# A two-layer kernel whose first layer takes its products for two batches in three rounded parts, in a new order of calls

## The reference

```
# layer 1, xn = layernorm(x)
q, k, v = xn Wq' + bq, xn Wk' + bk, xn Wv' + bv
attn = ((elu(q) + 1) * cumsum((elu(k) + 1) * v) / 4) Wo' + bo
xr = rms(xn) * norm_w;  logits = xr Wc' / temperature          # 512 logits for a token
w = softmax of the 32 largest logits;  e = sum of w * genes      # genes: 512 x 32
x = x + attn + tanh(e Wd') * xr * (e Wu') * scale
# layer 2, xn = layernorm(x)
q, k, v = rms(xn) w_qkv';  w = exp(rms(k))
y = sigmoid(rms(q)) * cumsum(w v) / (cumsum(w) + 1e-6)
u, g = y w_swiglu';  attn = xn + (u * silu(g)) w_out'           # 1024 wide inside
moe = sum over the 2 best of 16 experts of p * down(silu(gate) * up)   # 176 wide
      + a shared expert of the same form, 352 wide
x = x + attn + moe
```

## Time and profile before

| what | value |
|---|---|
| time, median of 3 runs | 539.07 us |
| the runs | 539.32, 539.07, 535.23 us |
| the profiled execution | 531.5 us |
| its span, from first to last instruction | 529.7 us |
| mean granted clock of PE | 0.994 of full speed |
| PE busy | 507.5 us, 96% of the span |
| DVE, ACT, POOL busy | 354.0, 296.0, 272.7 us |

### The profile page before, as it was taken

How to read it: one execution, slowest core, us unless ns; L and a number is a source line. 1 busy time by engine, 2 the same in 40 slices (tenths; PEclk the granted TensorE clock), 3 DMA queues, 4 the chain that set the end, 5 groups by cost and what they waited for, 6 DMA issues and landing times.

```text
span 529.7 us, 7444 instructions
## 1 busy us (share of the span) xinstructions
PE 507.5 (96%) x2488; PEld 384.8 (73%) x2488; DVE 354.0 (67%) x735; ACT 296.0 (56%) x577; POOL 272.7 (51%) x207
## 2 busy tenths in 40 slices
PE   7989999988999999999997999999999999999995
PEld 5565577766577766877885888887777777777684
DVE  4999995786998998847899895743232323323347
ACT  3788798785767758767653636225343343424321
POOL 0475648383472373383256346464576576666510
PEclk9999999998999999999999999999999999999999
DMA  8900031026020001037001850583322232223267
GB/s 271 372 6 1 1 124 37 0 100 220 1 80 40 1 1 41 1 129 243 1 1 44 292 179 14 187 232 98 108 91 89 71 100 83 97 80 89 71 242 265
DMA packets 19813, 54.32 MB, mean 103 GB/s; under 512 B 3312, under 2 KB 5792, under 8 KB 19776
## 3 DMA queue, kind: packets, MB, share of 16 engines
q1 hardware_dynamic: 15264, 41.52, 22.7%
q0 software_dynamic: 4512, 12.33, 7.7%
HBM read 36.14 MB, written 17.74 MB: 102 GB/s over the span
## 4 chain that ended last, share of the span: by engine, by line
PE 74%; DVE 15%; DMA 4%; issue 3%; ACT 2%; POOL 1%; SPq 1%; DVEq 0%; POOLq 0%; ACTq 0%
PE bank L280 52%; PE bank L442 9%; PE bank L355 3%; PE bank L474 2%; PE bank L501 2%; DMA fa<-in_x 2%; DMA ga<-y_rows 2%; DVE tk L972 1%; DVE m L970 1%; PE bank L328 1%; DVE fe L1029 1%; PE bank L400 1%; PE bank L292 1%; DVE tk L978 1%; DVE rw L1235 1%
## 5 line engine op out<-in xcount | busy, mean ns | idle before, releaser
L1214 DVE TENSOR_TENSOR m_h<-m_h,bank 128x176 f32<-128x176 f32 x47 | 15.8, 337 | 82.9 <-ACT m_h L789 82.9
L280 PE MATMUL bank<-mw,m_xt 128*128 x188 | 66.4, 476 | 0.2
L1362 POOL DMA_INDIRECT y_rows<-m_y,dest x47 | 46.9, 997 | 30.7 <-DVE m_y L1221 20.9
L1356 POOL DMA_INDIRECT xg<-xn_rows,tab x47 | 45.5, 969 | 28.0 <-PE bank L474 19.3
L280 PE MATMUL bank<-yhr,wsg_h 128*128 128x512 f32 x128 | 56.0, 437 | 0.8 <-ACT fc L721 0.8
L280 PE MATMUL bank<-hyr,wsg_h 128*128 128x512 f32 x128 | 50.1, 392 | 0.0
L280 PE MATMUL bank<-yhr,wsg_l 128*128 128x512 f32 x128 | 50.1, 391 | 0.0
L280 PE MATMUL bank<-mw,m_ht 88*128 x188 | 48.3, 379 | 0.0
L280 PE MATMUL bank<-fe,w_qkv 128*128 128x512 f32 x96 | 44.5, 594 | 0.6 <-ACT fe L622 0.6
L1347 POOL TENSOR_TENSOR hs0r<-hs,hq0r 128x512 fp32r<-128x512 f32 (+1 forms) x17 | 23.4, 1374 | 39.8 <-ACT hq0r L776 39.8
L280 PEld LDWEIGHTS bank<-mw,m_ht 88*128 88x128 f32 x188 | 35.2, 189 | 11.1 <-issue 0.4
...
## 6 DMA issues: line engine op xcount, KB each, us to landing
...
```

The source lines that it names most:

```text
L280: mm = e.matmul(o, a, b, start=n == 0, stop=n == len(terms) - 1)
L1214: e.tensor_tensor(m_h[j % 3][:, :], m_h[j % 3][:, :], ps("ju", j)[:, 176:352], ALU.mult).then_inc(s["jh"], 1)
L1356: e.indirect_dma_start(out=xg[j % 3][:, :], out_offset=None, in_=xn_d, in_offset=bass.IndirectOffsetOnAxis(ap=tab[:, j:j + 1], axis=0)).th ...
L1362: e.indirect_dma_start(out=y_d, out_offset=bass.IndirectOffsetOnAxis(ap=dest[:, j:j + 1], axis=0), in_=m_y[j % 3][:, :], in_offset=None).t ...
```

## The change

1. For batches 2 and 3 `project` and `logits` take three products of rounded parts instead of plain f32. The high parts of the weights (kv0h, q0h, wch) are made by `split(k)` on ACT, three calls of 128x1024, 128x512 and 128x1024; the low parts by `lows(k)` on POOL, three calls of the same sizes, written over the plain weights, so each waits until batches 0 and 1 have used these. xcopy1 rounds for these batches, and `lowx(b, h)` on DVE, four calls of 128x512, makes the low part, from turn1's bank, which is free only then.
2. The two exponentials get tiles of their own, three TS and two TE, in the room of the three TK and of what is left of them. `expert` of tile n now waits until tile n-2 is turned and totalled.
3. `awake` can take another bank; there are 55 idle products (10, 2, 12, 3, 3, 2, 4, 4, 9, 6) instead of 35 (10, 2, 2, 5, 4, 2, 8, 2).
4. refine waits for one semaphore instead of two; the returns of the spilled residual (rback) wait for batch 3's projections and logits, and eround for batch 2's or 3's, as they share room with the new parts.
5. All five lists of calls are in another order.

```diff
+        TS = [tile(f"tw{n}", 512) for n in range(3)]
+        TE = [tile(f"te{n}", 512) for n in range(2)]
+        qkv0_q = tile("qkv0_q", 512, F32R)
...
+        SPLITS = [(qkv0[:, :, D:768], kv0h, qkv0l[:, :, D:768]), (qkv0[:, :, 0:D], q0h, qkv0l[:, :, 0:D]), (wcv, wch, wcl)]
...
             def project(b, j, n, first, sem, back, key):
...
+                if b < 2:
+                    q.wait_ge(s["xc1"], 2 * b + 2)
+                    terms = [(qkv0[:, c, m * P:(m + 1) * P], FE[b % 2][:, c, :]) for c in range(2)]
+                else:
+                    q.wait_ge(s["xlo"], 2 * b - 2)
+                    q.wait_ge(s["wdr"], 4)
+                    terms = []
+                    for c in range(2):
+                        wh = kv0h[:, c, (m - 2) * P:(m - 1) * P] if first else q0h[:, c, m * P:(m + 1) * P]
+                        terms += [(wh, FEr[b % 2][:, c, :]), (qkv0l[:, c, m * P:(m + 1) * P], FEr[b % 2][:, c, :]), (wh, FGr[b % 2][:, c, :])]
...
+                    for c in range(2):
+                        h, l = FEr[b % 2][:, c, t], FGr[b % 2][:, c, t]
+                        terms += [(h, wch[:, c, :]), (h, wcl[:, c, :]), (l, wch[:, c, :])]
...
+            def split(k):
...
+                raw, h, _ = SPLITS[k]
+                e.activation(h, raw, ACT.Copy).then_inc(s["bor"], 1)
...
             def expert(b, i):
                 exponent()
                 n = 4 * b + i
-                if n > 2:
-                    q.wait_ge(s["emt"], n - 2)
+                if n > 1:
+                    q.wait_ge(s["emt"], n - 1)
+                    q.wait_ge(s["to"], n - 1)
...
+            def lowx(b, h):
+                q.wait_ge(s["wcs"], 2 * b - 2)
+                q.wait_ge(s["wv"], 2 * b - 2)
+                q.wait_ge(s["xc1"], 2 * b + h + 1)
+                t = slice(h * D, (h + 1) * D)
+                e.tensor_tensor(FGr[b % 2][:, :, t], ps("t1", b, h)[:, :].rearrange("p (c t) -> p c t", c=2), FEr[b % 2][:, :, t].bitcast(F32), ALU.subtract).then_inc(s["xlo"], 1)
...
+            def lows(k):
+
+                q.wait_ge(s["bor"], 4 + k)
+                for m, n in ((s["k"], 4), (s["v"], 4), (s["q"], 4 * (k == 1)), (s["lg"], 8 * (k == 2))):
+                    if n:
+                        q.wait_ge(m, n)
+                raw, h, l = SPLITS[k]
+                e.tensor_tensor(l, raw, h.bitcast(F32), ALU.subtract).then_inc(s["wdr"], 1)
```

More of the change, by code:

```diff
@@ L517, in tensor @@
-            ffn(1, 2, 0); dgate(0, 0, 4); ffn(1, 3, 3); dup(0, 0, 5); meank(0, 0); oproj(1, 0, 3); oproj(1, 1, 4); vproj2(0, 0, 5); vproj2(0, 1, 0)
-            dgate(0, 1, 2); ddown(0, 0, 6, 7); dup(0, 1, 1); turnr(1, 0, 3); turnr(1, 1, 4); dgate(0, 2, 5); qproj2(1, 0, 3); qproj2(1, 1, 0)
-            turn2(1, 0, 4); turn2(1, 1, 2); dup(0, 2, 1); meanq(1, 4); gates(1, 2); kproj2(1, 0, 5); kproj2(1, 1, 1); meank(1, 2); vproj2(1, 0, 4)
-            ddown(0, 1, 6, 7); vproj2(1, 1, 3); dgate(0, 3, 0); turn1(2, 0, 2); dup(0, 3, 5); logits(2, 0, 1); ddown(0, 2, 6, 7); logits(2, 1, 4)
@@ new lines, in tensor @@
+            dgate(0, 4, 2); turnr(1, 0, 4); turnr(1, 1, 1); dup(0, 4, 0); ddown(0, 2, 6, 7); turn1(2, 0, 4); qproj2(1, 0, 1); logits(2, 0, 3)
+            qproj2(1, 1, 4); turn2(1, 0, 5); logits(2, 1, 2); turn2(1, 1, 0); meanq(1, 5); dgate(0, 5, 0); ddown(0, 3, 6, 7); turn1(2, 1, 5)
+            kproj2(1, 0, 1); kproj2(1, 1, 4); logits(2, 2, 3); dup(0, 5, 5); meank(1, 0); vproj2(1, 0, 2); ddown(0, 4, 6, 7); kproj(2, 0, 5)
+            kproj(2, 1, 0); vproj2(1, 1, 1); dgate(0, 6, 5); emturn(2, 0, 4); logits(2, 3, 2); dup(0, 6, 0); ddown(0, 5, 6, 7); emturn(2, 1, 3)
@@ L1244, in vector @@
-            uptimes(1, 1); uptimes(1, 2); uptimes(1, 3); dtanh(0, 0); dtimes(0, 0); khat(0, 0); khat(0, 1); joined(1, 0); joined(1, 1); stats2(1)
-            wsum(0, 0); shift2(1); wsum(0, 1); divisor(0); gateb(0); wvtimes(0, 0); rlow(1, 0); wvtimes(0, 1); rlow(1, 1); wvsum(0, 0); wvsum(0, 1)
-            dtanh(0, 1); dtimes(0, 1); refine(0); dtanh(0, 2); dtimes(0, 2); gatea(1); qhat(1, 0); qhat(1, 1); gateb(1); stats1(2); khat(1, 0)
-            khat(1, 1); ratio1(2); wvtimes(1, 0); wvtimes(1, 1); wsum(1, 0); wvsum(1, 0); wsum(1, 1); divisor(1); topa(2, 0); wvsum(1, 1); topb(2, 0)
@@ L1256, in vector @@
-            rscale(3); uptimes(3, 0); gatea(2); dout(0, 1); uptimes(3, 1); uptimes(3, 2); uptimes(3, 3); qhat(2, 0); qhat(2, 1); joined(3, 0)
-            joined(3, 1); stats2(3); dtanh(1, 2); dtimes(1, 2); gateb(2); shift2(3); khat(2, 0); khat(2, 1); dtanh(1, 3); dtimes(1, 3); wvtimes(2, 0)
-            wvsum(2, 0); dtanh(1, 4); wsum(2, 0); wvtimes(2, 1); dtimes(1, 4); wsum(2, 1); wvsum(2, 1); divisor(2); dtanh(1, 5); gatea(3); gateb(3)
-            dtimes(1, 5); routea(); rlow(3, 0); dtanh(1, 6); rlow(3, 1); dtimes(1, 6); routeb(); qhat(3, 0); qhat(3, 1); dtanh(1, 7); dtimes(1, 7)
@@ L1272, in vector @@
[L1272 to L1275 removed]
+            statsh(); stats1(0); start(); ratio1(0); wcfold(); topa(0, 0); stats1(1); topb(0, 0); topa(0, 1); tope(0, 0); topb(0, 1); topf(0, 0)
@@ new lines, in vector @@
+            vtimes(1, 0); topg(1, 1); rlow(0, 0); rlow(0, 1); topb(1, 2); tope(1, 2); vtimes(1, 1); kvsum(1, 0); topf(1, 2); kvsum(1, 1); topg(1, 2)
+            qhat(0, 0); qhat(0, 1); topa(1, 3); topb(1, 3); qplus(1); tope(1, 3); topf(1, 3); topg(1, 3); khat(0, 0); khat(0, 1); wvtimes(0, 0)
+            wsum(0, 0); wvtimes(0, 1); wsum(0, 1); divisor(0); wvsum(0, 0); rscale(1); wvsum(0, 1); gatea(0); elow(1); dtanh(0, 0); uptimes(1, 0)
+            dtimes(0, 0); uptimes(1, 1); refine(0); dtanh(0, 1); uptimes(1, 2); uptimes(1, 3); dtimes(0, 1); dtanh(0, 2); dtimes(0, 2); joined(1, 0)
@@ new lines, in vector @@
+            joined(1, 1); stats2(1); shift2(1); stats1(2); ratio1(2); gateb(0); rlow(1, 0); rlow(1, 1); dtanh(0, 3); lowx(2, 0); dtimes(0, 3)
+            dtanh(0, 4); dtimes(0, 4); topa(2, 0); topb(2, 0); tope(2, 0); topa(2, 1); topb(2, 1); topf(2, 0); qhat(1, 0); qhat(1, 1); topg(2, 0)
+            tope(2, 1); lowx(2, 1); dtanh(0, 5); topf(2, 1); topa(2, 2); topg(2, 1); topb(2, 2); dtimes(0, 5); tope(2, 2); khat(1, 0); topf(2, 2)
+            khat(1, 1); topg(2, 2); wvtimes(1, 0); wsum(1, 0); kplus(2); wsum(1, 1); dtanh(0, 6); divisor(1); dtimes(0, 6); wvtimes(1, 1); wvsum(1, 0)
@@ new lines, in vector @@
+            khat(3, 1); onehot(5); wsum(3, 0); dtanh(2, 2); counts(); wsum(3, 1); dtimes(2, 2); divisor(3); dtanh(2, 3); dtimes(2, 3); onehot(6)
+            wvtimes(3, 0); wvtimes(3, 1); wvsum(3, 0); wvsum(3, 1); dtanh(2, 4); dtimes(2, 4); dtanh(2, 5); dtimes(2, 5); refine(3); dtanh(2, 6)
+            dtimes(2, 6); onehot(7); dtanh(2, 7); dtimes(2, 7); dtanh(2, 8); dtimes(2, 8); dtanh(2, 9); places(); table(); dtimes(2, 9); dtanh(2, 10)
+            dtimes(2, 10); dtimes(3, 0); dout(2, 0); dout(2, 1); dtimes(3, 1); dlow(3, 0); jtimes(0); jtimes(1); jtimes(2); jtimes(3); jout(0)
```

370 lines of the change are left out of this document (191 added, 179 removed), and 4 rows, old and new, of the table SIGNALS.

## The result

The changed kernel takes **554.71 us** (median, 552.08 to 555.9) against 539.2 us of the kernel before (535.23 to 540.48): **1.032 times as long, 95% interval 1.027 to 1.037**. The forecast was 531, its range ended at 542. The profiled execution of the kernel after took 554.54 us, its span is 552.7; that of before was 529.7, so the spans lie 23.0 us apart.

What follows compares the result with a forecast made beforehand. PE was taken as the bound, busy 507.5 of 529.7 us. Removed products -6.9, front -2.1 and routing +0.5 sum to -8.5 us, from the median 539.07 to 531; range 523 to 542.

Steps and rivals of the forecast that it cites:

- the removed work: Plain projections and logits of batches 2 and 3 on PE: 20 groups, 0.345 us less each, 6.9 us less work.
- walk: Call-by-call pass through the new lists up to dgate(0,3), with durations from the earlier trace; it put that start near 115.2.
- even at 123.7: Start of dgate(0,3), in us, at which the change would neither gain nor lose; each us later than 115.2 costs one.
- y of batch 0 returns no earlier: Rival: late DVE waits hold refine(0), so dgate(0,3) starts at 130.7 as before; +7.0 us, 546; chance 0.13.
- the one that the products are no faster: Rival: weight loads hold the twenty groups at 1.72 us; -1.6 us left, 537.5; its 0.02 within the first rival's chance.
- so I cost this at nothing there: Added rounding on ACT, POOL and DVE from 130.7 to 280: hidden in free engine time, 0 us.
- the front and DVE take part of it back: Rival: POOL's new subtractions hold up DVE ahead of PE; gain only 2.5 to 4.9 us, 534 to 536.5; chance 0.25.
- the term's own ceiling: Added rounding, if its cover is gone: at most the operations themselves, 0.7 to 2.7 us.
- a net 2.1 us: Front: dgate(0,3) starts 15.5 us earlier, but 13.4 us of batch 1's second-layer work now stands behind it.
- no PE wait over 1 us between 130 and 260: Sign to look for in the profile after, on PE's dense part behind the front, if the prediction holds.
- The idle products: 55 for 35 on PE, 0.43 us each, 8.6 us: 6.0 in the front, 2.6 at the routing.
- the last 26.6 us ... nothing in it is changed: Tail of returns and additions behind the last expert product: kept whole, no gain or loss.

Runs made afterwards that it cites:

- lows(2) alone: Changed kernel with POOL's lows(2) held until batch 1's second norm is through on DVE, nothing else held: 536.09 us, 1.010 to the kernel before.
- its hybrid: Changed kernel up to the first xturn, every engine's list in the order of the kernel before from there: 545.68 us, 1.015 to the kernel before.
- the last two kernels: Changed kernel with lows(2), prep(4), residual(3) held and six fewer idle products: 545.49 us, 1.014; the same with the old order from the first xturn: 539.26, 1.0036.

## Why the prediction was wrong

**What held.** The groups of parts are nearly as fast as read from the earlier trace rows: six of batch 1's second layer 1.37 us apart (134.76 to 136.13), the first logits of batch 2 from 133.30 to 134.76, 1.46. The mean of the twenty groups is 1.42, of the plain ones that went 1.69, so that the removed work is 5.5 us and not 6.9. The front's move came out nearly as walked: refine(0) at 104.94 (walk 100.2, bound 106), ylow's end at 117.12 (115.3), dgate(0,3) at 119.0 (115.2, even at 123.7, wrong from 122). lows(1) ended at 82.90, before the squares for kfold(0) at 84.92. The rival "y of batch 0 returns no earlier" is out, and so is the one that the products are no faster.

**The step that failed first: "so I cost this at nothing there", for the added rounding.** It was priced by the free time of engines over 150 us. What counts is which DVE step stands beside POOL's subtraction, and who waits for it. The rival "the front and DVE take part of it back" had the mechanism (its own terms give -2.4 to -4.4 us, not the -2.5 to -4.9 that stand there), but bounded each hold-up by the one in the earlier trace rows, 1.0 us, near the length of one POOL operation. The runs show that it isn't bounded by one operation: 5.87 us, through three. Its price by the experiments: 3.0 to 4.2 us for lows(2) alone, where the term's own ceiling was 2.7; and of the products' 6.9 us only 1.8 to 3.0 are left at the first xturn. The Trainium skill (SBUF — State Buffer, Who interferes with whom) has the shared port pair with one holder at a time; the traces agree, and go beyond what was drawn from it, in that the wait lasted until POOL had a gap.

**The second: "a net 2.1 us" for the front, and "no PE wait over 1 us between 130 and 260".** The move was summed only to dgate(0,3). The list behind it is new too, and it has waits of its own, three of over 1 us between 119 and 280 and two ahead of 52 us, which the walk's durations from before couldn't hold. Four of the five (35.38, 51.15, 126.19, 278.75) stand behind a DVE step lengthened by POOL; for the first it is the same kind of step as at 117.19, 128x4 in size:

```profile
32.87 1.23 DVE L928 SCALAR_TENSOR_TENSOR sm<-mv,sm 128x4 f32<-128x4 f32 x1
```

```profile
32.81 1.27 POOL L1358 TENSOR_TENSOR te<-te,tw 128x512 f32<-128x512 f32 x1 [1.69 <-ACT tw L721]
```

Only the one at 222.46 lies between 130 and 260. Expected were about -10 us of waits and lost clock up to the experts; PE's idle time rose by 2.5 and the low clock gave back 1.7. The idle products are the half of the sum that came true (9.5 us of PE's time, 8.6 forecast), and the gain that they were set against did not. Taken away they bring nothing, since the waits are there; with the waits mended, six fewer bring 0.4 us.

**The third: "the last 26.6 us ... nothing in it is changed", and beside it the experts' stage, taken over whole.** The tail held. The stage ahead of it, 286.1 to 503.1, was booked as 0.21 us of idle PE time that stays; but its order is written anew. On a chip without late starts that is worth about 1 us: 146.2 to 146.5 us in three kernels with the new order, 145.2 in one with the old, all on the same chip, and 145.6 in before's first trace. On the two with them it costs 4.5 to 6.2 us in timed runs (after against its hybrid; the last two kernels). The traces, one execution each, show less: 154.1 to 157.4 us in six with the new order (161.2 in after's first), 150.7 to 154.2 in four with the old, 2.8 us between the means. The late starts of over 0.5 us sum to 14.4 to 16.8 us in the new order and 9.6 to 13.6 in the old.

The sum had a sign of this. The profiled execution of before was 7.6 us quicker than the median, and I took these off evenly. They lie in this stage: 145.6 us there and 153.3 in the second trace of before, with the same 356.5 ahead of it. The forecast was made on a trace that didn't show what two of three chips do. (Which chips the first pair ran on is not recorded.)

**The sum again**, on the chips with late starts: 7.8 us up to the first xturn and 4.5 to 6.2 us for the order behind it are 12.3 to 14.0; after stood 13.0 to 15.5 above before in three timed pairs (550.22, 550.36 and 554.71). In the profiled pair 15.6 of 23.0 us lie in the stage, of which about 7.7 are before's own quick trace.

**What is open.** Where ACT's late starts come from. They come at the same calls in every trace of one order that has them (in before's, four traces: jxcopy 11, 24, 42 and 45, jhcopy 25; in after's, seven: jxcopy 12 and 33, jsilu 16, 21 and 32, jhcopy 31), not on every chip. The granted clock is 1.00 at the first of them each time, and the instruction traffic is the same with them and without (21 or 22 packets in queue q8, 16 in q14). That the step behind is late is shown; the cause is not. Of the waits up to the xturn, that at 35.38 (1.94) was not tested by a hold. That at 222.46 (1.23) isn't POOL's: the copy of ACT that ends it (L731, 221.83) stands in ACT's list behind steps of batch 2's second norm and a table load of 1.28 us. Of the kernels with this front only the one with plain products has no such wait. And the 3.8 us of PE's busy time beyond the count are taken apart only in part.
